# A Householder step with its pivot and divisor in one VectorE operation, and LSTM units in another order

## The reference

```python
L = jnp.diag(deg) - A
L_norm = d_inv_sqrt[:, None] * L * d_inv_sqrt[None, :]
_, U = jnp.linalg.eigh(L_norm)
agg = jnp.einsum('mn,bnd->bmd', U.T, features)
h = jax.nn.relu(agg @ W1 + b1)
out = jnp.einsum('nm,bmd->bnd', U, h @ W2 + b2)
...
for p in range(1, MAX_SKIP + 1):
    nw = Tv // p
    wins = h[:, :nw * p, :].reshape(Bv * nw, p, Hd)
    last = _lstm_last(Wih[p - 1], Whh[p - 1], bih[p - 1], bhh[p - 1], wins)
    idx = jnp.arange(nw) * p + (p - 1)
    h = h.at[:, idx, :].set(last.reshape(Bv, nw, Hd))
```

## Time and profile before

| what | value |
|---|---|
| median of 3 runs | 1600.31 us |
| the profiled execution: its time | 1604.85 us |
| its span, first to last instruction | 1603.0 us |
| outside the span | 1.85 us |
| busy over the span | PE 79%, DVE 78%, ACT 38%, POOL 25% |
| Householder stage, wide / narrow | 19.3 to 466.9 / 466.9 to 776.8 us |
| LSTM stage | 1266.5 to 1603.0 us |

### The profile page before, as it was taken

One profiled execution on the slowest core, in us unless ns is written; L12 is line 12 of the kernel. 1 busy time (PEld: TensorE's weight loads), 2 busy tenths in 40 slices (PEclk: granted clock), 3 DMA queues, 4 the chain that ended last, 5 costly groups with the idle time before them and its releaser, 6 DMA issues.

```text
span 1603.0 us, 25379 instructions
## 1 busy us (share of the span) xinstructions
PE 1272.1 (79%) x6001; PEld 1068.2 (67%) x6001; DVE 1246.9 (78%) x6154; ACT 610.2 (38%) x2116; POOL 397.3 (25%) x2138
## 2 busy tenths in 40 slices
PE   6999999999986667777354554365999999999997
PEld 5788888888875555555233333163778789999997
DVE  7999988888788888888899999996772345556555
ACT  1222222222233434322122222251334677878775
POOL 5333333434345555555200000002000010000000
PEclk9999999999999999999977776687999989999999
DMA  7000000000000000000000000000000000001001
GB/s 171 1 1 1 1 1 1 2 1 1 1 1 1 1 1 1 1 2 1 1 0 1 0 1 1 0 1 0 1 1 1 0 1 1 1 1 27 1 27 54
DMA packets 23404, 12.66 MB, mean 8 GB/s; under 512 B 5075, under 2 KB 22230, under 8 KB 23254
## 3 DMA queue, kind: packets, MB, share of 16 engines
q1 hardware_dynamic: 23254, 11.03, 2.8%
HBM read 6.83 MB, written 4.19 MB: 7 GB/s over the span
## 4 chain that ended last, share of the span: by engine, by line
DVE 46%; PE 37%; issue 8%; POOL 7%; ACT 2%; DVEq 1%; POOLq 0%
PE bank L824 8%; PE bank L826 5%; PE bank L833 4%; PE bank L669 4%; DVE A L1046 4%; DVE RC L1134 4%; DVE O L1142 4%; PE bank L672 3%; DVE pa L1130 3%; DVE O L1138 3%; PE pair L824 3%; DVE junk L993 2%; DVE zc L1040 2%; DVE wk L1030 2%; DVE O L1023 2%
## 5 line engine op out<-in xcount | busy, mean ns | idle before, releaser
L672 PEld LDWEIGHTS bank<-O 128*128 128x128 f32 x764 | 201.5, 344 | 0.0
L681 PE MATMUL bank<-O,y 128*128 128x2 f32 x510 | 142.6, 349 | 64.4 <-DVE y L993 59.7
L614 ACT ACTIVATE H<-bank,gate_b 128x128 f32<-128x128 f32 (+2 forms) x468 | 163.3, 434 | 59.0 <-PE bank L826 40.6
L669 PE MATMUL bank<-ident,O 128*128 128x128 f32 x382 | 148.1, 457 | 46.6 <-DVE O L1023 35.6
L477 ACT ACTIVATE ncp<-pc,RC 128x2 f32<-128x2 f32 (+1 forms) x254 | 74.9, 295 | 283.5 <-DVE RC L1014 283.5
L681 PEld LDWEIGHTS bank<-O,y 128*128 128x128 f32 x510 | 129.5, 314 | 75.1 <-issue 72.2
L672 PE MATMUL bank<-O 128*128 128x1 f32 x764 | 162.8, 305 | 0.0
L824 PE MATMUL bank<-O,WlT 128*128 128x128 f32 (+1 forms) x672 | 146.9, 328 | 7.8 <-DVE O L1410 5.6
L689 PE MATMUL pair<-ident,pc 128*128 128x128 f32 x381 | 147.7, 457 | 5.6 <-DVE pc L1012 2.2
L669 PEld LDWEIGHTS bank<-ident,O 128*128 128x128 f32 x382 | 60.2, 198 | 134.4 <-DVE O L1023 134.4
L473 ACT ACTIVATE root<-bank 128x1 f32<-128x1 f32 x255 | 43.7, 171 | 259.8 <-PE bank L672 259.8
(11 more groups left out here) (431 smaller groups left out, 3321.9 us busy)
## 6 DMA issues: line engine op xcount, KB each, us to landing
X<-in_x SPq DMA_DIRECT2D x2, 2048.0 KB, 13.1
out<-X SPq DMA_DIRECT2D x32, 128.0 KB, 1.9
adj_sb<-in_adj SPq DMA_DIRECT2D x1, 256.0 KB, 3.0
W1s<-in_L_gnn_W SPq DMA_DIRECT2D x1, 64.0 KB, 11.1
W2s<-in_L_gnn_W SPq DMA_DIRECT2D x1, 64.0 KB, 4.2
Wg0s<-in_L_gnn_Wg SPq DMA_DIRECT2D x1, 64.0 KB, 3.9
Wg1s<-in_L_gnn_Wg SPq DMA_DIRECT2D x1, 64.0 KB, 3.9
Wl<-in_L_gnn_Wih SPq DMA_DIRECT2D x1, 0.5 KB, 6.7
```

The costliest lines, as they stand in the source:

```text
L614: ins = a(gates[:, q, i, 0:n], gate_at(p, q, i), fn, bias=gate_b[:, p - 1, i:i + 1])
L669: ins = nc.tensor.transpose(xb[:, b * P:(b + 1) * P], R[:, b, k, 0:1].to_broadcast([P, P]), idf)
L672: ins = mm(bank[0][:, 0:1], R[:, b, k, 0:1].to_broadcast([P, P]), R[:, b, k, 0:1], start=(b == bl[0]), stop=(b == 1))
L681: ins = mm(sb_[:, 0:2], y[:, 1:2].to_broadcast([P, P]), R[:, 1, k, :], start=True, stop=(k >= P - 1))
```

## The change

In the Householder step, `half` gets a second column, half * x0 (a new VectorE operation, placed behind L993 and ahead of L1001). sigma moves to column 1 of bank 0, and column 0 is set to zero once. One scalar_tensor_tensor then makes both: NG = half * root - (0, sigma), in the place of pb and g1. `tm` becomes one VectorE operation, tm = ym * RC0 + tmp (the seed is now added unscaled), where cx stood; cx moves to GpSimd in the place of sy, yb and tm.

In the LSTM stage `FIRST` lists eight groups that go ahead of everything (all of set 0's p = 1 and 2, most of set 1's, one of set 2), and `TURN` a round that is laced with later sets. The transposes back and the additions to X move from (set, 4, 2) to (set, 4, 1), the last four additions are spread over the last units, and the cells of p = 1 get buffers of their own.

```diff
-    ORDER = ((1, 0, 0), (3, 0, None), (1, 0, 1), (3, 1, None), (3, 2, None), (4, 0, None),
-             (2, 0, None), (4, 1, None), (2, 1, None), (4, 2, None), (4, 3, None))
+    FIRST = ((0, (1, 0, 0)), (0, (1, 0, 1)), (1, (1, 0, 0)), (0, (2, 0, None)), (1, (1, 0, 1)), (0, (2, 1, None)), (1, (2, 0, None)), (2, (1, 0, 0)))
+    TURN = ((0, (3, 0, None)), (1, (2, 1, None)), (0, (3, 1, None)), (0, (3, 2, None)), (2, (1, 0, 1)), (0, (4, 0, None)),
+            (3, (1, 0, 0)), (0, (4, 1, None)), (0, (4, 2, None)), (2, (2, 0, None)), (0, (4, 3, None)))
...
-                    pool.wait_ge(S["pb_ready"], k + 1)
-                    g.tensor_tensor(sy[:, bs], tmp[:, bs, c0 + 1], pb.to_broadcast([P, w]), ALU.mult).then_inc(S["sy_ready"], 1)
-                    pool.wait_ge(S["sy_ready"], k + 1)
-                    g.tensor_tensor(yb[:, bs], ym[:, bs], sy[:, bs], ALU.add).then_inc(S["yb_ready"], 1)
-                    pool.wait_ge(S["yb_ready"], k + 1)
+                    pool.wait_ge(S["xm_ready"], k + 1)
                     pool.wait_ge(S["c_ready"], k + 1)
-                    g.tensor_tensor(tm[:, bs], yb[:, bs], RC[:, k, 0:1].to_broadcast([P, w]), ALU.mult).then_inc(S["t_ready"], 1)
+                    g.tensor_tensor(cx[:, bs], xm[:, bs], RC[:, k, 1:2].to_broadcast([P, w]), ALU.mult).then_inc(S["cx_ready"], 1)
...
-                tt(pb, root[:], half[:], ALU.mult).then_inc(S["pb_ready"], 1)
-                if not last:
-                    dve.wait_ge(S["xm_ready"], k + 1)
+                stt(out=NG[:, k, :], in0=half[:], scalar=root[:], in1=zs, op0=ALU.mult, op1=ALU.subtract).then_inc(S["pb_ready"], 1)
                 dve.wait_ge(S["pb_ready"], k + 1)
-                stt(out=NG[:, k, 1:2], in0=pb, scalar=x0, in1=sigma, op0=ALU.mult, op1=ALU.subtract).then_inc(S["g1_ready"], 1)
...
+                dve.wait_ge(S["ym_ready"], k + 1)
                 dve.wait_ge(S["c_ready"], k + 1)
-                tt(cx[:, bs], xm[:, bs], nc_.to_broadcast([P, w]), ALU.mult).then_inc(S["cx_ready"], 1)
+                stt(out=tm[:, bs], in0=ym[:, bs], scalar=prn, in1=tmp[:, bs, c0 + 1], op0=ALU.mult, op1=ALU.add).then_inc(S["t_ready"], 1)
...
-                if u < NU and (p, t) == (4, 2) and gr:
+                if u < NU and (p, t) == (4, 1) and gr:
                     residual(SLOTS * (gr - 1) + q, 2 * q + 1)
-            for q in range(SLOTS):
-                residual(PAIRS - SLOTS + q, 2 * q + 1)
+                if u > NU - SLOTS + 1:
+                    q = u - NU + SLOTS - 2
+                    residual(PAIRS - SLOTS + q, 2 * q + 1)
+            residual(PAIRS - 1, 2 * SLOTS - 1)
```

More of the change, by code:

```diff
@@ L53, in gnn_kernel @@
     SLOTS = 4
-    ORDER = ((1, 0, 0), (3, 0, None), (1, 0, 1), (3, 1, None), (3, 2, None), (4, 0, None),
-             (2, 0, None), (4, 1, None), (2, 1, None), (4, 2, None), (4, 3, None))
     SETS = PAIRS // SLOTS
[L57 to L62, removed]
+    FIRST = ((0, (1, 0, 0)), (0, (1, 0, 1)), (1, (1, 0, 0)), (0, (2, 0, None)), (1, (1, 0, 1)), (0, (2, 1, None)), (1, (2, 0, None)), (2, (1, 0, 0)))
+    TURN = ((0, (3, 0, None)), (1, (2, 1, None)), (0, (3, 1, None)), (0, (3, 2, None)), (2, (1, 0, 1)), (0, (4, 0, None)),
+            (3, (1, 0, 0)), (0, (4, 1, None)), (0, (4, 2, None)), (2, (2, 0, None)), (0, (4, 3, None)))
+    UNITS = [(gr, un, q) for gr, un in FIRST for q in range(SLOTS)]
+    for r in range(SETS):
+        UNITS += [(r + ahead, un, q) for ahead, un in TURN if r + ahead < SETS for q in range(SLOTS)]
     AT = {unit: u for u, unit in enumerate(UNITS)}
@@ L108, in gnn_kernel @@
         drow = sb("drow", [P, N]); sq = sb("sq", [P, 2])
-        root = sb("root", [P, 1]); half = sb("half", [P, 1]);
+        root = sb("root", [P, 1]); half = sb("half", [P, 2])
         NG = sb("NG", [P, N, 2]); RC = sb("RC", [P, N, 2]); sh = sb("sh", [P, N])
@@ L115, in gnn_kernel @@
         y = sb("y", [P, 2]); ym = sb("ym", [P, 2]); tm = sb("tm", [P, 2]); pc = sb("pc", [P, 2]); ncp = sb("ncp", [P, 2])
-        xm = sb("xm", [P, 2]); cx = sb("cx", [P, 2]); zc = sb("zc", [P, 2]); sy = sb("sy", [P, 2]); yb = sb("yb", [P, 2]); vt = sb("vt", [P, 2])
+        xm = sb("xm", [P, 2]); cx = sb("cx", [P, 2]); zc = sb("zc", [P, 2]); vt = sb("vt", [P, 2])
         gqn = sb("gqn", [P, 1]); kc = sb("kc", [P, 1]); wk = sb("wk", [P, 1])
@@ L182, in gnn_kernel @@
             lt_rdy adjT_rdy adjT_cp wlt_ps wlt_cp biases
-            x_ready xrow_ready sig_ready root_ready g1_ready y_part y01_ready y0_ready y1_ready half_ready pb_ready p_ready c_ready
-            xm_ready ym_ready vt_ready v_ready kc_ready ncp_ready sy_ready yb_ready t_ready s_ready prow0_ready prow1_ready cx_ready gq_ready w_ready z_ready add0 add1 upd0 upd1 s_hist d0_ready seed_rdy half_upd
+            x_ready xrow_ready sig_ready root_ready y_part y01_ready y0_ready y1_ready half_ready hx_ready pb_ready p_ready c_ready
+            xm_ready ym_ready vt_ready v_ready kc_ready ncp_ready t_ready s_ready prow0_ready prow1_ready cx_ready gq_ready w_ready z_ready add0 add1 upd0 upd1 s_hist d0_ready seed_rdy half_upd
             ln_sum ln_mean ln_var ln_root ln_rstd ln_shift ln_norm
@@ L222, in cell_at @@
         def cell_at(p, q, n):
-            return (Vh, VT)[q // 2][:, q % 2, 0:n] if p <= 2 else cell[:, q, 0:n]
+            if p == 1:
+                return (Pm, Rm)[q // 2][:, q % 2, 0:n]
+            return (Vh, VT)[q // 2][:, q % 2, 0:n] if p == 2 else cell[:, q, 0:n]
         def hst_at(p, q, n):
@@ L472, in _ @@
                 act.wait_ge(S["sig_ready"], k + 1)
-                a(root[:], bank[0][:, 0:1], ACT.Sqrt, scale=4.0).then_inc(S["root_ready"], 1)
+                a(root[:], bank[0][:, 1:2], ACT.Sqrt, scale=4.0).then_inc(S["root_ready"], 1)
                 if not last:
@@ L671, in _ @@
                 for b in bl:
-                    ins = mm(bank[0][:, 0:1], R[:, b, k, 0:1].to_broadcast([P, P]), R[:, b, k, 0:1], start=(b == bl[0]), stop=(b == 1))
+                    ins = mm(bank[0][:, 1:2], R[:, b, k, 0:1].to_broadcast([P, P]), R[:, b, k, 0:1], start=(b == bl[0]), stop=(b == 1))
                 ins.then_inc(S["sig_ready"], 1)
@@ L899, in give_back @@
                 last.then_inc(S["tr_ps"], 1)
+            given = [0] * SLOTS
             for u, (gr, (p, t, part), q) in enumerate(UNITS):
@@ L913, in _ @@
                         pe.wait_ge(S["third_rdy"], gr + 1)
-                    if part == 0 and gr >= 3:
-                        pe.wait_ge(S["out_add"], SLOTS * (gr - 3) + q + 1)
+                    if p != 4 and given[q]:
+                        pe.wait_ge(S["out_add"], given[q])
                     gate_products(u)
-                if (p, t) == (4, 2) and gr:
+                if (p, t) == (4, 1) and gr:
                     give_back(c - SLOTS, 2 * q + 1)
+                    given[q] = c - SLOTS + 1
             for q in range(SLOTS):
@@ L951, in _ @@
             link(tt(deg[:], rs[:], bank[0][:, 0:2], ALU.add))
+            v.memset(bank[0][:, 0:1], 0.0)
             link(ts(pos[:], deg[:], 0.0, None, ALU.is_gt))
@@ L984, in _ @@
                 x0, s_, y0_ = xb[:, c0:c0 + 1], sb_[:, 0:1], sb_[:, 1:2]
-                sigma = bank[0][:, 0:1]
+                zs = bank[0][:, 0:2]
                 pb, prn, nc_ = NG[:, k, 0:1], RC[:, k, 0:1], RC[:, k, 1:2]
                 dve.wait_ge(S["xrow_ready"], k + 1)
-                ts(half[:], x0, 0.0, 0.5, ALU.is_lt, ALU.subtract).then_inc(S["half_ready"], 1)
+                ts(half[:, 0:1], x0, 0.0, 0.5, ALU.is_lt, ALU.subtract).then_inc(S["half_ready"], 1)
                 for b in reversed(bl):
@@ L997, in _ @@
                     v.reciprocal(rstd[:], rstd[:]).then_inc(S["ln_rstd"], 1)
+                dve.wait_ge(S["half_ready"], k + 1)
+                tt(half[:, 1:2], half[:, 0:1], x0, ALU.mult).then_inc(S["hx_ready"], 1)
                 if b0 == 0:
@@ L1012, in _ @@
                     stt(out=pc[:, bs], in0=A[:, bs, c0], scalar=pb, in1=y[:, bs], op0=ALU.mult, op1=ALU.subtract, reverse1=True).then_inc(S["p_ready"], 1)
-                dve.wait_ge(S["g1_ready"], k + 1)
                 v.reciprocal(RC[:, k, :], NG[:, k, :]).then_inc(S["c_ready"], 1)
```

4 lines of the change are left out of this document (2 added, 2 removed).

## The result

The changed kernel takes 1598.53 us (median of 20 runs, 1597.54 to 1599.31); the kernel before, run beside it, 1601.82 us (20 runs, 1599.38 to 1605.01). The ratio is 0.9978 with a 95% interval of 0.9971 to 0.9985: 3.3 us less, where 7.9 were forecast. It moved the way that was forecast and lies in the wide range (1582 to 1602), but outside the forecast's own range of 1588 to 1597, and the size did not hold. The 7.9 were counted from the median of three runs, 1600.31 us; with 20 runs that median is 1.5 us higher. The profiled execution of the changed kernel took 1598.64 us, its span 1596.8, so it lies at its own median.

A forecast was written before the change was run, and what follows sets the result against it. Householder steps were taken as bound by chains between engines, the LSTM stage by TensorE, with only its pauses to win. 1604.85 us profiled + 3.9 - 11.8 = 1597.0, less 4.5 to the median: 1592.4 us, own range 1588 to 1597, wide 1582 to 1602.

The forecast's parts named there:

- both stretches at the lower clock: LSTM stage: TensorE's slow-clock time behind its two longest pauses, forecast to go, 1.7 and 2.7 us.
- Wide steps: Householder steps before the narrow ones: -0.05 us each in steps 56 to 126, -0.5 us for the earlier 56; -4.1 us.
- The chain: Wide step, y's first half through pair, pc, reciprocal, tm and gqn to x: 1.23 or 1.24 us instead of 1.29.
- The first 56: Early wide steps, taken as set by the matrix update and product s, which do not move: -0.5 us in all.
- Narrow steps: Later Householder steps: half * x0 is exposed behind the accumulator read, +0.14 us a step at first, falling later; +8 us.
- LSTM and end: LSTM stage and final stores: pauses and slow clock removed, a new pause and slower ScalarE units added; -11.8 us.
- both long pauses: TensorE's LSTM waits for hidden states of (0, 1, b), 2.1 us, and GpSimd's copies, 3.5 us; both forecast to go.
- the new pause: LSTM stage: (1, 4, 1) follows (1, 4, 0) at once, so TensorE waits; 1.9 us taken between zero and 4.
- Rival 1: Householder step: tm's second wait is free, tm starts 0.04 behind the reciprocal; -9.8 us, 1582.6 us; chance 0.10.
- Rival 2: Narrow steps: half * x0 is free beside the accumulator read, -1 instead of +8 us; 1583.4 us; chance 0.10.
- Rival 3: Householder step: pc waits 0.10 us for the pair instead of 0.04; +15 us, 1607.6 us; chance 0.13.
- Rival 4: LSTM stage: slow clock stays at the start (+4.4 us) and follows the new pause (+2.2 us); 1599.0 us; chance 0.15.

The follow-up runs named there:

- e3: The kernel before, without any edit, profiled a second time; this execution took 1603.6 us.
- e4: The kernel before, without any edit, profiled a third time; this execution took 1600.04 us.
- e1: The changed kernel with the old LSTM order put back, so the Householder part alone; 1608.14 us, ratio 1.0041 to the kernel before.
- e2: The changed kernel with the old Householder step put back, so the LSTM part alone; 1592.84 us, ratio 0.9945 to the kernel before.
- e6: The changed kernel with only tm's two waits written in the other order; 1585.43 us, ratio 0.9895 to the kernel before.
- e5: The changed kernel with the old operations (pb, g1, cx on VectorE; sy, yb, tm on GpSimd) in narrow steps alone; 1587.7 us, ratio 0.9909.
- e9: e5's kernel with the waits of VectorE's two-wait operations ordered by stage, the one fulfilled last written first; 1563.21 us, ratio 0.9752.
- e8: e2's kernel with the two waits of pb, g1, x, zc and y's first half turned in all steps; 1589.47 us, ratio 0.992.
- e10: e9's kernel with the two waits of TensorE's product s (L686) in the other order; 1560.54 us, ratio 0.9735.

## Why the prediction was wrong in size

**The step that failed** is the last one: "That execution stands 4.5 us over the median of the runs shown, so the prediction is 1592.4 us." It carries the distance of one execution of the kernel before over to the changed kernel. But the sum had already taken away both stretches at the lower clock (1.7 and 2.7 us), and e3, e4 and e1 show that these come and go from execution to execution behind the same pauses. 2.5 us of the distance lie in the LSTM part that the change removes, and these were counted twice; 1.5 us are the error of a median of three runs; 0.5 stay unplaced. The changed kernel's profiled execution lies at its own median, so none of the 4.5 us carried over. The sum before that step, 1597.0 us, misses the measured 1598.5 by 1.5 us. That remaining miss is the Householder stage, +5.6 us instead of +3.9. What I should have taken is the sum without the distance, since most of its cause stood in the terms; against the median of before the LSTM part is then 9.3 us (e2) and not 11.8.

**Wide steps**: -5.1 us against -4.1 forecast. The chain was right, tm's own length and the handover behind it were mis-sized by 0.02 us together: steps 56 to 126 gave -2.8 (forecast -3.6), from the starts of L988 before and L987 after. The first 56 gave -2.3 (forecast -0.5, bounds 0 and -2.8), 0.04 us a step like the later ones, so they are not held by what doesn't move, as I took. The price of a single step scatters, though, and I haven't followed these.

**Narrow steps**: +10.7 us against +8. By stretch, with the forecast behind it: steps 127 to 164 +5.9 (5.3), to 201 +3.4 (3.4), to 219 +0.5 (0.3), the last 34 +1.0 (-0.5). In the last stretch tm is a part: at k = 202 pair to x is 1.12 us (655.70 to 656.82), where 1.10 was forecast and 1.11 stood before. That is 0.02 of the 0.04 us that each of these steps missed by; the rest is not shown. And the sum of the parts, 8.5, had been rounded down to 8. Householder together: +5.6 against +3.9, in the timed runs +6.0 (e1).

**LSTM and end**: -11.8 us between the two profiled executions, -11.8 forecast. The parts are in the trace: both long pauses gone with their stretches, two 1.4 us pauses instead of four, a new one of 1.7 (1.9 forecast) before (1, 4, 1), the end 1.6 shorter (1.5). The pauses (11.2 to 4.5 us), the clock (4.4) and the end add to -12.7, so 1.0 us the other way is not placed; the forecast had +0.6 there, for ScalarE's slower units. That the new pause came out so near its 1.9 is luck in part: it was a choice between zero and 4.

**Rivals.** Rival 1 (the second wait is free) is false as it was stated, tm starts 0.10 behind the reciprocal; e6 shows what is true in it: written in the other order it costs 0.03. (Its price was 9.8 us, e6 gained 13.1.) Rival 2 is refuted by the narrow stage, +10.7 us against its -1, and by k = 134, where the pair starts 0.18 behind the read and pb had started with it. Rival 3 is refuted by pc, 0.03 behind the pair. Rival 4 came out near in size, but its mechanism is absent: the clock is 1.00 throughout, and no stretch at the lower level follows the new pause.

What stays open is why a pause of 2.1 or 3.5 us is followed by the lower clock in one execution and not in another, and why an operation is recorded 0.03 us longer when its late wait is the second. For the longer handover itself the traces show the instruction in between, not why the wait written second is the one that becomes it.

## What to carry to other kernels

Before the distance between a profiled execution and the median is added to a forecast, find out where it lies: profile the unchanged kernel once or twice more and compare the stages. If the change removes what varies, the distance goes with it. And in a chain of short operations, look at which of an instruction's two waits is fulfilled last and write that one first; in this kernel this was worth 24.5 us (e5 to e9) with no operation on data changed, seven times what the whole change gave; turned without looking it cost 7.0 us in e8's wide steps.

## What was not expected of the hardware

- Of an instruction's two waits, the late one costs 0.03 to 0.05 us if it is written first in the program and 0.10 to 0.11 if second, on VectorE; on TensorE 0.06 and 0.15 from the read of y (e10, e9). The one written second is an instruction of its own (21 ns on VectorE, 51 ns on TensorE).
- A VectorE operation on 2 elements of each partition lasts 0.25 us with its late wait second and 0.22 with it first (the changed kernel and e6, k = 76), and the next one starts 0.17 to 0.19 behind it in both.
- The same pauses of TensorE of 2.1 and 3.5 us went with 3.4 and 6.8 us, with 3.4 and 0, and with 0 and 0 us at the lower clock in three executions of one kernel.
